# Decoder layer on one core: the last three output tiles moved one step ahead

## Chip, cores and metric

The kernel runs on one core of a Trainium2 chip. The metric is device time in microseconds (us). Besides the timed runs there is one profiled execution, from which the rows and stretches below are read. TensorE is called PE in the profile, VectorE DVE, ScalarE ACT, GpSimd POOL and SyncE SP.

## What is computed

One post-norm decoder layer for x of (2, 512, 1024), that is 1024 rows in 8 tiles of 128 rows:

```python
x = _layernorm(x + attention(x, wq, wk, wv, wo))       # 32 query heads, 8 key/value heads, window of 128
x = _layernorm(x + matmul(fake_quant(x), fake_quant(ctx)))   # "cross product"; quantised to 0..255
x = _layernorm(x + ffn(x, w_gate, w_up, w_down))       # gate and up products, truncated, down product
```

The change sits where the attention's output product (`@ wo.T`) of the last head group ends, and the first layernorm, the quantised cross product and the second layernorm follow.

## The kernel before

Each engine has its program written out by hand, and engines wait for one another with semaphores; each engine works through its own list in order. After the last attention group the 8 row tiles go through a pipeline of steps that the code calls slots: `slot(2)` to `slot(13)`. Each of the four compute engines has its own function `slot(i)`.

**TensorE**, L1224 and on. `out_tile(t)` is the last head group's output product of tile t: 24 matmuls of 128x512 in float32 (two halves of 12, L1118 to L1120), into PSUM banks 6 and 7. Its half waits until VectorE has added the same half of the tile before (`y_added`). `turn_x2(t)` transposes the second layernorm's result (8 transposes, L1220), `turn_quantised(t)` the quantised rows (8, L1188), and `cross(t)` makes the sums over each row (8 matmuls of one column, L1201) and then the cross product (16 matmuls in bf16, L1207). In slot i stand, in this order, `out_tile(i+1)` (slots 3 to 6), `turn_x2(i-6)` (from 6), `turn_quantised(i-2)` and `cross(i-3)`. So output tiles 4, 5, 6 and 7 stand in slots 3, 4, 5 and 6. From slot 11 on, parts of the feed-forward's gate and up products (L1284, L1285) stand between the slots, and behind slot 13 these products follow one another.

**VectorE**, L2765 and on. In slot i: `cross_add(i-4)` (L2718, waits for `cross(i-4)`), the small steps of the first layernorm's scale for tile i-1 (`ln_link(0, i-1, ...)`), among them the statistics of the second layernorm of tile i-4 (`ln_half(1, i-4, ...)`, L2679, and `ln_variance`), then `add_half(i+1, half)` for both halves (L2499, slots 3 to 6), the small steps of tile i-4 (from L2697), the first layernorm's statistics of tile i (which wait for its adds) and `round_rows(i-1)` (L2711). From slot 10 on `mix_columns(i-6)` (L2744 to L2751) is behind that.

**ScalarE**, `slot(i)` to slot 5 and `fast_slot(i)` from 6. In slot 6: `root(1, 2)` (L1719, waits for the variance from VectorE), `normed(0, 5)` (L1725, waits for the first layernorm's scale), `left_high(0)` (L1770, copies what `turn_x2(0)` made), `row_shift(3)` (L1749, waits for the row sums of `cross(3)`), `scale_rows(5)` (L1736), `copy_turned(4)` (L1742), `left_whole(0)` (L1774), `root(0, 6)` and `normed(1, 2)`. In slot 7 `left_high(1)` and `copy_turned(5)` stand first, then `root(1, 3)`, `normed(0, 6)`, `row_shift(4)`, `scale_rows(6)`, `left_whole(1)`, `root(0, 7)` and `normed(1, 3)`. `turn_x2(1)` on TensorE waits for `left_whole(0)`, which frees the banks that it writes. `round_rows(5)` on VectorE waits for `scale_rows(5)`.

**GpSimd** in slot i: `quantise_rows(i-2)` (L2208, waits for `round_rows(i-2)`; `turn_quantised(i-2)` on TensorE waits for it), `xb_l` of tile i-7 (L2224, from slot 7), the context's sums added to tile i-2 (L2244), and the row shift added to tile i-3 (L2250, waits for `row_shift(i-3)`; `cross_add(i-3)` waits for it).

**SyncE** waits for all output products (`wo_done`) before it loads `jw`, stores each finished tile of the second layernorm (`keep_x2`) and loads the weights of the feed-forward behind these stores.

Slot 6 and later stand in a branch (`FIRST_SLOT = 6`), which is chosen by a value that VectorE makes in slot 3.

Of the kernel before, what the change touches and what calls it, by code (L numbers as in the profile page):

```python
# [18 lines left out]
TILES = TOK // P  # L19
# [12 lines left out]
NH = DM // HALF  # L32
# [38 lines left out]
def build(nc, x_rows, x_cols, w_att, ctx_rows, x1_scale, x1_zp, x2_scale, x2_zp, w_gu, w_down, out):  # L71
    with ExitStack() as stack:
# [609 lines left out]
        def ln_of(k, t):  # L682


            return ln[:, k % 2 * 2 + t % 2, :]
# [297 lines left out]
        def _(pe):  # L983
# [128 lines left out]
            def out_product(m, into, t, half):  # L1112

                b, rows = t // TPB, slice(t % TPB * P, (t % TPB + 1) * P)
                for h in range(GROUP):
                    oh = o_h[b][:, h, rows]
                    ol = o_l[b][:, h, rows]
                    pe.matmul(into, oh, wo_h[half][:, h, :], start=(h == 0), stop=False)  # L1118
                    pe.matmul(into, oh, wo_l[half][:, h, :], start=False, stop=False)  # L1119
                    last = pe.matmul(into, ol, wo_h[half][:, h, :], start=False, stop=(h == GROUP - 1))  # L1120
                last.then_inc(wo_done, 1)
# [18 lines left out]
            def out_tile(t):  # L1140

                if t == TPB:
                    pe.wait_ge(o_low, HKV * UNITS)
                for half in range(NH):
                    m = OUT_BLOCKS - 2 * (TILES - t) + half
                    pe.wait_ge(y_added, m - 1)
                    out_product(m, y_ps[1 + half], t, half)
# [34 lines left out]
            def turn_quantised(t):  # L1182
                pe.wait_ge(x_quant, t + 1)
                if t == 0:
                    pe.wait_ge(p_low, HKV * UNITS)
                wait(pe, xq_ready, t)
                for c in range(DC):
                    last = pe.transpose(turned_bf[:, c * P:(c + 1) * P], x_q[:, t % 2, c * P:(c + 1) * P], ident_bf[:, :])  # L1188
                last.then_inc(xq_turned, 1)

            def cross(t):

                pe.wait_ge(xq_ready, t + 1)
                if t == 0:
                    pe.wait_ge(o_low, HKV * UNITS)
                    pe.wait_ge(y_added, OUT_BLOCKS - 12)
                    pe.wait_ge(sum_ready, 1)
                    pe.wait_ge(path_chosen, 1)
                wait(pe, shift_ready, t)
                for c in range(KC):  # L1200
                    last = pe.matmul(bank(5)[:, 0:1], x_qt[:, t % 2, c, :], ones_bf[:, 0:1],  # L1201
                                     start=(c == 0), stop=(c == KC - 1))
                last.then_inc(rows_summed, 1)
                wait(pe, cross_added, t)
                for half in range(NH):
                    for c in range(KC):
                        last = pe.matmul(bank(half), x_qt[:, t % 2, c, :],  # L1207
                                         ctx_quantised((t // TPB) * KC + c)[:, half * HALF:(half + 1) * HALF],
                                         start=(c == 0), stop=(c == KC - 1))
                last.then_inc(cross_done, 1)  # L1210

            def turn_x2(t, general):
                pe.wait_ge(ln_done[1], t + 1)
                wait(pe, x2_copied, t if general else min(t, TPB))
                if not general:
                    wait(pe, x2_taken, t - TPB)
                if t == 0:
                    pe.wait_ge(sum_ready, BATCH)
                for c in range(DC):
                    last = pe.transpose(bank(2 + c // 4)[:, (c % 4) * P:(c % 4 + 1) * P],  # L1220
                                        resid[:, t, c * P:(c + 1) * P], ident[:, :])
                last.then_inc(x2_turned, 1)

            def slot(i, general=False):  # L1224


                if 3 <= i < TILES - 1:
                    out_tile(i + 1)
                if 6 <= i < TILES + 6:
                    turn_x2(i - 6, general)  # L1230
                if 2 <= i < TILES + 2:
                    turn_quantised(i - 2)
                if 3 <= i < TILES + 3:
                    cross(i - 3)
# [33 lines left out]
            out_tile(3)  # L1268
            values_pair(g, 6)
            slot(2)  # L1270
            sum_context(1, 0)
            sum_context(1, 1)
# [1083 lines left out]
        def _(dve):  # L2356
# [139 lines left out]
            def add_product(m, source, t, half):  # L2496
                cols = slice(half * HALF, (half + 1) * HALF)
                dve.wait_ge(wo_done, m + 1)
                dve.tensor_tensor(resid[:, t, cols], source, resid[:, t, cols], ALU.add).then_inc(y_added, 1)  # L2499
# [9 lines left out]
            def add_half(t, half):  # L2509
                add_product(OUT_BLOCKS - 2 * (TILES - t) + half, y_ps[1 + half], t, half)  # L2510
# [178 lines left out]
            def ln_link(k, t, i):  # L2689

                if 0 <= t < TILES:
                    small = ln_of(k, t)
                    mean, var, root, r0 = small[:, 12:13], small[:, 14:15], small[:, 15:16], small[:, 16:17]
                    sq, corr, inv, offset = small[:, 17:18], small[:, 18:19], small[:, 19:20], small[:, 20:21]
                    if i == 0:
                        dve.wait_ge(ln_root[k], t + 1)
                        dve.reciprocal(r0, root).then_inc(ln_step[k], 1)  # L2697
                    else:
                        dve.wait_ge(ln_step[k], t * LN_STEPS + 3 + i)
                    if i == 1:  # L2700
                        dve.tensor_scalar(sq, r0, r0, var, ALU.mult, ALU.mult).then_inc(ln_step[k], 1)
                    if i == 2:
                        dve.tensor_scalar(corr, sq, -0.5, 1.5, ALU.mult, ALU.add).then_inc(ln_step[k], 1)
                    if i == 3:
                        dve.tensor_scalar(inv, r0, corr, None, ALU.mult).then_inc(ln_step[k], 1)
                    if i == 4:
                        dve.tensor_scalar(offset, mean, inv, -1.0, ALU.mult, ALU.mult).then_inc(ln_scale[k], 1)
# [6 lines left out]
            def cross_add(t):  # L2714

                dve.wait_ge(cross_done, t + 1)
                dve.wait_ge(x1_moved, t + 1)
                dve.scalar_tensor_tensor(out=resid[:, t, :], in0=ps[:, 0:2, :].rearrange("p a n -> p (a n)"),  # L2718
                                         scalar=param(S12), in1=resid[:, t, :], op0=ALU.mult,
                                         op1=ALU.add).then_inc(cross_added, 1)  # L2720
                dve.wait_ge(cross_added, t + 1)

            def choose_path():

                dve.wait_ge(misfit_sum, 1)
                dve.tensor_scalar(general[:, :], bank(0)[:, 0:1], 1.0, None, ALU.min).then_inc(path_chosen, 1)
# [30 lines left out]
            def slot(i, general=False):  # L2757

                if i == 3:
                    choose_path()  # L2760
                if 4 <= i < TILES + 4:
                    cross_add(i - 4)
                ln_link(0, i - 1, 0)
                ln_half(1, i - 4, 0)
                ln_link(0, i - 1, 1)  # L2765
                ln_half(1, i - 4, 1)
                ln_link(0, i - 1, 2)
                ln_variance(1, i - 4)
                if i == 3:
                    context_sums(1)  # L2770
                ln_link(0, i - 1, 3)
                for half in range(NH):
                    if 3 <= i < TILES - 1:
                        add_half(i + 1, half)
                    if half == 0:
                        ln_link(0, i - 1, 4)
                ln_link(1, i - 4, 0)
                if i < TILES:
                    dve.wait_ge(y_added, TILE_ADDED[i])
                ln_half(0, i, 0)  # L2780
                ln_link(1, i - 4, 1)
                ln_half(0, i, 1)
                ln_link(1, i - 4, 2)
                ln_variance(0, i)
                ln_link(1, i - 4, 3)
                ln_link(1, i - 4, 4)
                if 1 <= i < TILES + 1:
                    round_rows(i - 1)
                if general and LOW_BY_POOL + 6 <= i < TILES + 6:
                    columns_low(i - 6)  # L2790
                if not general and TPB + 6 <= i < TILES + 6:
                    mix_columns(i - 6)
# [335 lines left out]
```

## Time and profile before

| | |
|---|---|
| median of 3 runs | 1472.59 us (1471.60 to 1473.77) |
| profiled execution, its own time | 1474.21 us |
| its span, first to last instruction | 1472.5 us |
| TensorE busy | 1431.7 us (97%) |
| VectorE busy | 1002.9 us (68%) |
| ScalarE busy | 791.0 us (54%) |
| GpSimd busy | 740.1 us (50%) |
| mean granted clock of TensorE | 0.995 |

Busy shares are means over the whole span. The span is made of stages with different limits; the slots of the change take about 90 us of it, from 1027 to 1117 us. All times below that look like 1061.21 are counted from the start of the span. A row of the timeline is: start in us, length in us, engine, line, operation, what it writes and reads, how many of them follow one another, and in square brackets how long the engine had been idle before it and which instruction ended that. Matmuls overlap, so a group's length is a little over its distance to the next.

### The profile page before, as it was taken

To read this page: it belongs to the slowest core of one execution; us is meant where nothing else is said; L and a number is where in the kernel's file an instruction comes from. 1 tells how busy PE (TensorE), PEld (TensorE's weight loads), DVE (VectorE), ACT (ScalarE), POOL (GpSimd) and SP (SyncE) were. 2 spreads that over 40 slices of the span, in tenths; PEclk is the share of its full clock that TensorE was granted. 3 is DMA by queue.
4 is the path that set the end of the run, shared out by engine and by line. 5 is a ranking of instruction groups with operands and counts; after the bars stand their busy time and mean duration, and the time that the engine had idled before them with its cause. 6 is when DMAs were issued, how large, how long until landed. Compare 5 with 4: busy or idle time off the path is not lost.

```text
span 1472.5 us, 22884 instructions
## 1 busy us (share of the span) xinstructions
PE 1431.7 (97%) x7072; PEld 1158.4 (79%) x7088; DVE 1002.9 (68%) x1768; ACT 791.0 (54%) x1561; POOL 740.1 (50%) x651
## 2 busy tenths in 40 slices
PE   8899999999999999999999999999979999999996
PEld 6688888888888888888888888887648888778643
DVE  7644444445555578888888888887787656556596
ACT  5433333333345465657566666674576555555674
POOL 0477777777566445555555555553475333443100
PEclk9999999999999999999999999999999999999998
DMA  6378777777662757576767676671131222122611
GB/s 228 140 272 285 285 282 268 275 273 261 208 236 101 297 181 280 178 264 195 269 205 264 217 256 230 223 267 76 38 149 59 93 100 87 70 92 86 230 43 73
DMA packets 105882, 281.10 MB, mean 191 GB/s; under 512 B 12768, under 2 KB 13152, under 8 KB 105824
## 3 DMA queue, kind: packets, MB, share of 16 engines
q1 hardware_dynamic: 105824, 280.41, 54.1%
q8 instruction: 27, 0.44, 0.1%
q14 instruction: 31, 0.25, 0.1%
HBM read 184.94 MB, written 95.42 MB: 190 GB/s over the span
## 4 chain that ended last, share of the span: by engine, by line
PE 54%; DVE 6%; ACT 3%; issue 2%; DMA 2%; POOL 1%; SPq 1%; DVEq 0%; ACTq 0%; POOLq 0%
PE ps L1118 8%; PE ps L1120 7%; PE ps L1119 7%; PE ps L1284 6%; PE ps L1285 6%; PE ps L1337 5%; PE ps L1048 2%; PE ps L1047 2%; PE ps L1049 2%; PE ps L1060 2%; PE ps L1095 2%; PE ps L1094 2%; PE ps L1096 2%; PE ps L1207 1%; DVE u_val L2829 1%
## 5 line engine op out<-in xcount | busy, mean ns | idle before, releaser
L1028 PE MATMUL ps<-xo_h,wb_h 128*128 128x512 f32 x644 | 251.6, 391 | 6.0 <-ACT c L1502 2.8
L1029 PE MATMUL ps<-xo_l,wb_h 128*128 128x512 f32 x644 | 250.7, 389 | 0.0
L1030 PE MATMUL ps<-xo_h,wb_l 128*128 128x512 f32 x644 | 250.7, 389 | 0.0
L1118 PE MATMUL ps<-wo_h,o_h 128*128 128x512 f32 x512 | 207.9, 406 | 1.8 <-DMA wo_l<-wo_low 1.8
L1120 PE MATMUL ps<-wo_h,o_l 128*128 128x512 f32 x512 | 200.3, 391 | 0.0
L1119 PE MATMUL ps<-wo_l,o_h 128*128 128x512 f32 x512 | 200.1, 391 | 0.0
L2156 POOL TENSOR_TENSOR pm_l<-pt_l,upto 128x512 fp32r<-128x512 f32 x58 | 74.8, 1290 | 230.4 <-DVE pt_l L2480 230.4
L1497 ACT ACTIVATE wb_h<-wf_l 128x512 fp32r<-128x512 f32 x69 | 43.6, 632 | 197.8 <-DVE wf_l L2409 82.3
L1028 PEld LDWEIGHTS ps<-xo_h,wb_h 128*128 128x128 f32 x644 | 120.9, 188 | 33.8 <-issue 6.0
L2121 POOL TENSOR_TENSOR wb_l<-wf_l,wb_h 128x512 fp32r<-128x512 f32 x66 | 88.8, 1346 | 112.8 <-DVE s_sum L2404 56.8
L1546 ACT ACTIVATE prob<-prob,exp_bias 128x128 f32<-128x128 f32 x256 | 99.8, 391 | 83.5 <-DVE exp_bias L2467 83.5
L1030 PEld LDWEIGHTS ps<-xo_h,wb_l 128*128 128x128 f32 x644 | 120.9, 188 | 25.4
L1029 PEld LDWEIGHTS ps<-xo_l,wb_h 128*128 128x128 f32 x644 | 120.9, 188 | 24.6
L2121 POOL TENSOR_TENSOR wb_l<-raw,wb_h 128x512 fp32r<-128x512 f32 x66 | 88.1, 1336 | 62.5 <-DVE wb_l L2393 48.5
L1120 PEld LDWEIGHTS ps<-wo_h,o_l 128*128 128x128 f32 x512 | 96.1, 188 | 21.5
L1118 PEld LDWEIGHTS ps<-wo_h,o_h 128*128 128x128 f32 x512 | 96.5, 188 | 19.2 <-DMA wo_l<-wo_low 1.3
L2499 DVE TENSOR_TENSOR resid<-ps,resid 128x512 f32<-128x512 f32 x128 | 87.5, 684 | 32.7 <-PE ps L1120 31.3
L1119 PEld LDWEIGHTS ps<-wo_l,o_h 128*128 128x128 f32 x512 | 96.6, 189 | 16.5
L2137 POOL TENSOR_TENSOR q_l<-q_raw,q_h 128x512 fp32r<-128x512 f32 x64 | 83.1, 1298 | 16.3 <-ACT q_h L1524 16.3
L1284 PE MATMUL ps<-t_h,ws 128*128 128x512 f32 x228 | 88.7, 389 | 0.0
L1285 PE MATMUL ps<-t_l,ws 128*128 128x512 f32 x228 | 88.7, 389 | 0.0
L2132 POOL TENSOR_TENSOR wp_l<-wp_raw,wp_h 128x1024 fp32r<-128x1024 f32 x32 | 76.8, 2400 | 0.0
(262 smaller groups left out, 3579.0 us busy)
## 6 DMA issues: line engine op xcount, KB each, us to landing
raw<-w_att SPq DMA_DIRECT2D x47, 512.0 KB, 5.4
f_raw<-w_gu SPq DMA_DIRECT2D x44, 512.0 KB, 5.0
u_gu<-f_unit SPq DMA_DIRECT2D x42, 512.0 KB, 5.0
gq<-u_gu SPq DMA_DIRECT2D x42, 512.0 KB, 3.8
wp_raw<-w_att SPq DMA_DIRECT2D x32, 512.0 KB, 5.9
wo_high<-wp_h SPq DMA_DIRECT2D x32, 512.0 KB, 2.8
wo_low<-wp_l SPq DMA_DIRECT2D x32, 512.0 KB, 4.1
q_rows<-c SPq DMA_DIRECT2D x64, 256.0 KB, 2.9
```

The source lines that it names most:

```text
L1028: pe.matmul(prod_ps[i], wh, chunk(xo_h[i], c), start=(i in OPENS and c == 0), stop=False, skip_group_check=True)
L1029: pe.matmul(prod_ps[i], wh, chunk(xo_l[i], c), start=False, stop=False, skip_group_check=True)
L1030: last = pe.matmul(prod_ps[i], wl, chunk(xo_h[i], c), start=False, stop=(c == KH - 1), skip_group_check=True)
L1118: pe.matmul(into, oh, wo_h[half][:, h, :], start=(h == 0), stop=False)
L1119: pe.matmul(into, oh, wo_l[half][:, h, :], start=False, stop=False)
L1120: last = pe.matmul(into, ol, wo_h[half][:, h, :], start=False, stop=(h == GROUP - 1))
L1284: pe.matmul(dst, w[:, c * P:(c + 1) * P], chunk(xh, c), start=(start and c == 0), stop=False, skip_group_check=True)
L1285: last = pe.matmul(dst, w[:, c * P:(c + 1) * P], chunk(xl, c), start=False, stop=(c == KH - 1), skip_group_check=True)
L1546: last = act.activation(prob[:, par, a, :], prob[:, par, a, :], ACT.Exp, bias=exp_bias[:, par, a:a + 1], scale=SCALE, accum_out=row_sum[:, ...
L2121: pool.tensor_tensor(wb_l[i][:, :], weight_source(odd, i), plain(wb_h[i][:, :]), ALU.subtract).then_inc(w_low, 1)
L2137: pool.tensor_tensor(q_l[:, j % 2, :], q_raw[:, :], plain(q_h[:, j % 2, :]), ALU.subtract).then_inc(q_low, 1)
L2499: dve.tensor_tensor(resid[:, t, cols], source, resid[:, t, cols], ALU.add).then_inc(y_added, 1)
```

## The change

On TensorE slot 3 issues `out_tile(4)` and also `out_tile(5)`, slot 4 `out_tile(6)`, slot 5 `out_tile(7)`, and slot 6 none. On VectorE slot 3 adds tile 4 where it did, and tile 5 a little further down; slots 4 and 5 add tiles 6 and 7 there, behind the first small step of the second layernorm; slot 6 adds none. ScalarE, GpSimd and SyncE keep their programs. The number of instructions, their shapes and the buffers are the same.

```diff
@@ TensorE, slot(i) @@
-                if 3 <= i < TILES - 1:
-                    out_tile(i + 1)
+                if i == 3:
+                    out_tile(4)
+                if 3 <= i < TILES - 2:
+                    out_tile(i + 2)
                 if 6 <= i < TILES + 6:
                     turn_x2(i - 6, general)
@@ VectorE, slot(i) @@
                 for half in range(NH):
-                    if 3 <= i < TILES - 1:
-                        add_half(i + 1, half)
+                    if i == 3:
+                        add_half(4, half)
                     if half == 0:
                         ln_link(0, i - 1, 4)
                 ln_link(1, i - 4, 0)
+                if 3 <= i < TILES - 2:
+                    for half in range(NH):
+                        add_half(i + 2, half)
                 if i < TILES:
                     dve.wait_ge(y_added, TILE_ADDED[i])
                 ln_half(0, i, 0)
```

## Rows read from the trace of the kernel before

**Rows 1.** The page, busy time of each engine.
```profile
PE 1431.7 (97%) x7072; PEld 1158.4 (79%) x7088; DVE 1002.9 (68%) x1768; ACT 791.0 (54%) x1561; POOL 740.1 (50%) x651
```

**Rows 2.** PE's waits, 1000 to 1250 us: total, times, longest.
```profile
PE ps L1220 <- DVE x_l L2751: 4.3, 2, 3.9
PE ps L1220 <- ACT xb_raw L1774: 3.8, 3, 1.9
PE ps L1188 <- POOL x_q L2208: 0.4, 1, 0.4
```

**Rows 3.** Chain that ended last, in order of time: start, us, what.
```profile
1062.95 3.41 PE ps L1207 x15
1066.38 1.29 DVE resid L2718
...
1071.45 1.14 ACT x_scaled L1736
...
1074.40 2.36 POOL xb_l L2224
...
1083.02 4.78 PE ps L1207 x15
```

**Rows 4.** Timeline of PE: out_tile(4) with what follows, out_tile(7), slots 6, 7, 12.
```profile
1026.92 0.48 PE L1118 MATMUL ps<-wo_h,o_h 128*128 128x512 f32 x1
...
1032.47 0.62 PE L1188 MATMUL ps<-ident_bf,x_q 128*128 128x128 bf16 x8
...
1055.55 0.58 PE L1118 MATMUL ps<-wo_h,o_h 128*128 128x512 f32 x1
...
1061.21 1.03 PE L1220 MATMUL ps<-ident,resid 128*128 128x128 f32 x8
...
1066.56 1.06 PE L1220 MATMUL ps<-ident,resid 128*128 128x128 f32 x8 [0.21 <-ACT xb_raw L1774]
...
1105.48 1.23 PE L1220 MATMUL ps<-ident,resid 128*128 128x128 f32 x8 [3.91 <-DVE x_l L2751]
```

**Rows 5.** Timeline of DVE, slots 5 to 8.
```profile
1054.67 0.68 DVE L2711 TENSOR_SCALAR x_scaled<-x_scaled 128x1024 f32<-128x1024 f32 x1
1055.94 1.28 DVE L2718 SCALAR_TENSOR_TENSOR resid<-ps,prm,resid 128x1024 f32<-128x1024 f32 x1 [0.58 <-PE ps L1207]
...
1066.38 1.28 DVE L2718 SCALAR_TENSOR_TENSOR resid<-ps,prm,resid 128x1024 f32<-128x1024 f32 x1 [1.07 <-PE ps L1207]
...
1069.95 0.15 DVE L2697 RECIPROCAL ln<-ln 128x1 f32<-128x1 f32 x1
...
1072.62 0.69 DVE L2711 TENSOR_SCALAR x_scaled<-x_scaled 128x1024 f32<-128x1024 f32 x1 [0.34 <-ACT x_scaled L1736]
1073.23 1.28 DVE L2718 SCALAR_TENSOR_TENSOR resid<-ps,prm,resid 128x1024 f32<-128x1024 f32 x1
```

**Rows 6.** Timeline of ACT, slots 6 and 7.
```profile
1059.26 0.20 ACT L1719 ACTIVATE ln<-ln 128x1 f32<-128x1 f32 x1 [3.22 <-DVE ln L2687]
...
1062.28 1.02 ACT L1770 ACTIVATE xb_h<-ps 128x1024 fp32r<-128x1024 f32 x1 [0.94 <-PE ps L1220]
...
1063.35 1.24 ACT L1736 ACTIVATE x_scaled<-resid,prm 128x1024 f32<-128x1024 f32 x1
...
1065.38 1.03 ACT L1774 ACTIVATE xb_raw<-ps 128x1024 f32<-128x1024 f32 x1
...
1067.66 1.02 ACT L1770 ACTIVATE xb_h<-ps 128x1024 fp32r<-128x1024 f32 x1
...
1069.69 0.20 ACT L1719 ACTIVATE ln<-ln 128x1 f32<-128x1 f32 x1
1070.07 1.24 ACT L1725 ACTIVATE resid<-resid,ln 128x1024 f32<-128x1024 f32 x1 [0.17 <-DVE ln L2707]
...
1074.74 1.02 ACT L1770 ACTIVATE xb_h<-ps 128x1024 fp32r<-128x1024 f32 x1
```

**Rows 7.** Timeline of POOL: quantise_rows(4).
```profile
1055.44 1.05 POOL L2208 TENSOR_SCALAR x_q<-x_scaled 128x1024 bf16<-128x1024 f32 x1 [1.49 <-DVE x_scaled L2711]
```

**Rows 8.** Busy by stretch: PE, PEld, DVE, ACT, POOL, PE's granted clock, DMA share, GB/s.
```profile
1083.00:1086.00 3.00, 2.98 (x8) 1.16 (x8) 1.62 (x8) 2.78 (x5) 3.00 (x2) 0.54 0.46 171
...
1105.50:1110.00 4.50, 4.50 (x17) 3.79 (x18) 3.19 (x4) 2.18 (x4) 4.50 (x3) 0.62 0.00 0
```

## Prediction

> **What bounds the kernel now.** I read the page first: TensorE is busy for 97% of the span [rows 1], so time can only be won or lost in its few idle stretches or in what it must do. The change moves no work between engines and adds none, so the question is what it does to TensorE's idle time. The second view is the list of TensorE's waits around the change: from 1000 to 1250 us there are some 8.5 us of them, nearly all in front of `turn_x2`, for ScalarE's copy that frees its banks and for VectorE's `mix_columns`, and one for GpSimd's quantised rows [rows 2]. None falls before 1061 us: slots 3 to 5 are dense on TensorE. The third view is the chain that ended last. It stays on TensorE through `cross(3)`, leaves it at 1066.38 us for VectorE's `cross_add(3)`, and then runs over ScalarE's `scale_rows(6)` and GpSimd's `xb_l` back to TensorE's `cross(6)` at 1083.02 us [rows 3]. So up to slot 6 TensorE sets the pace, and in slots 7 to 12 the other three do. From `turn_x2(6)` at 1105.48 us on, before which it waited 3.91 us [rows 4], TensorE is dense again. What is late at that point is late at the end, and what is early there is won. The timelines of slots 6 and 7 [rows 4 to 7] then give the step.
>
> **Slots 3 to 5, TensorE.** An output tile takes 5.55 us (1026.92 to 1032.47) [rows 4]. The 24 matmuls of `out_tile(5)` go in front of `cross(0)`, so `cross(0)`, `cross(1)` and `cross(2)` each end about 5.5 us later. I take 5.5. No wait appears there, by my reading: `out_tile(5)` needs tile 4's first half added, an add that VectorE can make while TensorE is on the second half. When `out_tile(7)` is done, TensorE has done the same instructions in both versions, so `turn_x2(0)` starts at 1061.2 us as it does now [rows 4]. For TensorE alone the swap costs nothing and brings nothing; its cover is that these slots have no waits.
>
> **Slots 4 to 6, VectorE.** Its adds wait for the output tiles and its `cross_add` for the cross products, so its slots 4 and 5 keep their pattern and lie 5.5 us later. `cross_add(2)`, which opens slot 6, moves from 1055.94 [rows 5] to 1061.4. `round_rows(4)` moves from 1054.67 [rows 5] to 1060.15, and `quantise_rows(4)` from 1055.44 to 1060.9 and ends at 1062.0 [rows 7], just when TensorE comes to `turn_quantised(4)` (0.9 us behind 1061.2). That costs 0 to 0.1; I take 0. `cross(3)` then ends near 1066.3 as now.
>
> Slot 6 of VectorE has no adds any more. A slot without adds is slot 7, from 1066.38: ScalarE's `root(1, 3)` follows 3.31 us behind its start (1069.69), `normed(0, 6)` 3.69 us (1070.07), and its `round_rows` would be at 5.83 (5.90, unless ScalarE is late; it stood at 6.24 with 0.34 of waiting) [rows 5, 6]. I use 3.69 and 5.9.
>
> **Slot 6, ScalarE: here the change costs.** Now `root(1, 2)` starts at 1059.26 and `normed(0, 5)` just behind it, both before TensorE's transposes are there, and `left_high(0)` follows at 1062.28 [rows 6]. After the change `normed(0, 5)` can't start before 1061.4 + 3.69 = 1065.1. ScalarE's list is fixed, so `left_high(0)`, `row_shift(3)`, `scale_rows(5)`, `copy_turned(4)` and `left_whole(0)` queue up behind it. With `normed` taking 1.24 [rows 6], `left_high(0)` starts at 1065.1 + 1.24 = 1066.33: 1066.33 - 1062.28 = 4.05 us later. From there to slot 7's `left_high(1)` at 1067.66 ScalarE is dense, so everything in it is 4.05 us later: `scale_rows(5)` starts at 1067.4 and ends at 1068.64; `left_whole(0)` starts at 1069.4; `left_high(1)` at 1071.7. Who waits: `turn_x2(1)` on TensorE goes from 1066.56 to 1070.6, so TensorE sits idle from 1066.2 for some 4.4 us (now 0.21) [rows 4]; `round_rows(5)` goes to 1068.7, so `cross_add(3)` is at 1069.3 against 1066.38 [rows 5], 2.9 us later.
>
> **Slot 7 brings the two delays together.** `root(1, 3)` stands behind `left_high(1)` and `copy_turned(5)`: 1071.7 + 1.82 = 1073.5. VectorE needs it 3.57 us into its slot (1069.95 - 1066.38) [rows 5], that is at 1072.9, and waits. ScalarE's `normed(0, 6)`, on the other hand, need no longer wait for VectorE. Now it starts 0.38 behind `root(1, 3)` [rows 6]; two that don't wait follow at about 0.12, as the root is short. So it starts at 1073.65 against 1070.07: 3.6 us later. `scale_rows(6)`, `round_rows(6)`, `cross_add(4)` (1076.8 against 1073.23 [rows 5]) and `left_high(2)` (1078.3 against 1074.74 [rows 6]) all hang on this with the pattern of now. From here both engines and GpSimd are late by one amount, the loop through the three is closed, and I see nothing in slots 8 to 12 with slack against it.
>
> **The other parts.** SyncE's `jw` load waits for the last output product, now 4 us earlier; it is used 50 us later. GpSimd's list does not change; its slot 7 work (xb_l, sums, shift) ends before `round_rows(6)` is there. Bank waits of the two output tiles back to back: 0, or at most the length of an add, under them the 5.5 us of a tile.
>
> **The sum:** 0 (slots 3 to 5) + 4.05 (slot 6, ScalarE) - 0.45 (slot 7, ScalarE's own waits on VectorE that go) = +3.6 us. Against the profiled execution's own 1474.21 that is 1477.8; it stands 1.6 above the median of the runs, so against 1472.59 it is 1476.2 us.
>
> **TensorE's clock** is a term of both signs. After the idle 3.91 us before `turn_x2(6)` the granted clock was 0.62 over the next 4.5 us, and in slot 9, behind several short waits, 0.54 over 3 us [rows 4, 8]: each a stretch at 1.2 GHz instead of 2.4. In slot 9 the 15 matmuls took 4.78 where slot 6's took 3.41 [rows 3], 1.4 us on the chain. The new idle 4.4 us can bring such a stretch into slot 7. By the same two rows it costs nothing if it ends before `turn_x2(1)`, and 1.4 or a little more, say 1.7, if all of it is on the path; its first instructions, the transposes, are on it and the cross product behind them has over 1 us of room, so I put 0.9 there as likely if it comes. On the other side, shifted waits in slot 9 may leave the clock at full and give 1.4 back. I take the two as cancelling, and keep the ends -1.4 and +1.7.
>
> The Trainium skill (TensorE: Matmul & The Clock Gate, "What's actually happening" and "HAM oscillation") says that an idle stretch that is long enough brings TensorE back to half its clock, and that sustained work must pass before it is lifted. The trace agrees in the 0.62 behind the 3.91 us [rows 4, 8]. By that rule this change speaks against itself, since it makes a gap of the same length in slot 7: the sum would be 3.6 + 0.9 = 4.5 us.
>
> **The rivals.**
> (a) The half clock falls into slot 7 and slot 9 keeps its own: +4.5, up to 3.6 + 1.7 = +5.3, so 1477.1 to 1477.9. For it: the length of the gap. Against: only what follows at once is on the path. 20%.
> (b) Not slower: TensorE stays at full clock through slots 7 and 9. Then 3.6 - 1.4 = +2.2, 1474.8 us, within 0.2%. It decides where the stretch of slot 9 goes and costs under 0.7 in slot 7. For it: slot 9's stretch came from several small waits, and these shift. Against: the pattern of the waits stays as it is. 17%.
> (c) Only VectorE counts, since ScalarE catches up: slot 6 of VectorE takes 6.5 us without waits, `cross_add(3)` stands at 1061.4 + 6.5 = 1067.9, 1.5 us later than now: 1474.1. Against it: ScalarE's list is dense for 6 us behind a start that is 5 us later. 9%.
> (d) Faster: with no output tile in slot 6, its cross product is done earlier and the slots behind gain. It would need slot 5 to end early, but that now holds the tile. The most it could bring is the 1.07 that VectorE waited for `cross(3)` [rows 5] and slot 9's 1.4, some 2.5 us or 1470; a gain over 0.2% needs more than this. 4%.
>
> **How the numbers follow.** About 0.2%, 2.9 us, is what a measurement of this kernel can tell from no change. The forecast of +3.6 (3.0 to 4.4) has 50% and (a) 20%; both lie above that bound. (b) and (c) are within 0.2%, 26%, and (d) holds 4%. The forecast is near the bound, so I move 3 of its 50 to "same". Faster 4%, same 29%, slower 67%. The range reaches from (c), 1474.0, to past (a), 1478.4.
>
> **What would show it.** In the profile after: `turn_x2(0)` near 1061 as before; `cross_add(2)` near 1061.4; ScalarE with no idle time from about 1065 to 1072; TensorE idle for about 4 us in front of `turn_x2(1)`, its wait named as ScalarE's `xb_raw`; `turn_x2(6)` near 1109. I am wrong if TensorE waits in slots 3 to 5, if `left_high(0)` is not behind `normed(0, 5)` in time, or if the delay shrinks between slots 7 and 12.

## The result: 0.28% slower

The changed kernel takes 1477.83 us (median of 13 runs, 1475.77 to 1480.05), the kernel before in the same rounds 1473.59 us. The ratio is 1.0028 with a 95% interval of [1.0021, 1.0035], that is 4.1 us with 3.1 to 5.2. The forecast was 1476.2 us, 3.6 above a median of 1472.59 for the kernel before; that median came out 1.0 higher in these rounds, so the difference is the better comparison. Differences in us are the ratio's part above 1 times the median before; one of the 11 executions of experiment 1 took 1796.67 us and is left out of its ratio.

**The profile after.** TensorE's waits from 1000 to 1250 us (engine, line, released by: total, times, longest), which answer to [rows 2]:

```profile
PE ps L1220 <- ACT xb_raw L1776: 6.4, 2, 4.1
PE ps L1220 <- DVE x_l L2753: 4.2, 2, 3.9
PE ps L1207 <- DVE resid L2720: 0.8, 2, 0.5
```

The wait for `mix_columns` is as long as it was. The wait for ScalarE's copy has grown from 3.8 to 6.4, and its longest from 1.9 to 4.1. Of the third row, 0.46 are new: `cross(3)` waits for `cross_add(2)`. The timeline of TensorE shows where (`turn_x2(0)`, `cross(3)`, `turn_x2(1)` with what follows in slot 7, and `turn_x2(6)`), beside [rows 4]:

```profile
1026.31 0.48 PE L1118 MATMUL ps<-wo_h,o_h 128*128 128x512 f32 x1
...
1060.58 1.04 PE L1220 MATMUL ps<-ident,resid 128*128 128x128 f32 x8
...
1062.69 3.63 PE L1207 MATMUL ps<-ctx_q,x_qt 128*128 128x512 bf16 x16 [0.46 <-DVE resid L2720]
1070.43 1.94 PE L1220 MATMUL ps<-ident,resid 128*128 128x128 f32 x8 [4.12 <-ACT xb_raw L1776]
1072.17 1.06 PE L1188 MATMUL ps<-ident_bf,x_q 128*128 128x128 bf16 x8
...
1073.28 4.84 PE L1207 MATMUL ps<-ctx_q,x_qt 128*128 128x512 bf16 x16
...
1109.85 1.89 PE L1220 MATMUL ps<-ident,resid 128*128 128x128 f32 x8 [3.87 <-DVE x_l L2753]
```

`turn_x2(0)` starts 34.3 us behind the start of `out_tile(4)` in both kernels (1060.58 - 1026.31 and 1061.21 - 1026.92): slots 3 to 5 cost TensorE nothing. `turn_x2(1)` then waits 4.12 us for `left_whole(0)`. Its 8 transposes take 1.94 us where [rows 4] have 1.06, and the cross product behind them 4.84.

ScalarE in slots 6 and 7, beside [rows 6]:

```profile
1064.66 0.20 ACT L1721 ACTIVATE ln<-ln 128x1 f32<-128x1 f32 x1 [3.83 <-DVE ln L2689]
1065.03 1.24 ACT L1727 ACTIVATE resid<-resid,ln 128x1024 f32<-128x1024 f32 x1 [0.17 <-DVE ln L2709]
1066.18 1.00 ACT L1772 ACTIVATE xb_h<-ps 128x1024 fp32r<-128x1024 f32 x1
...
1067.23 1.24 ACT L1738 ACTIVATE x_scaled<-resid,prm 128x1024 f32<-128x1024 f32 x1
...
1069.26 1.03 ACT L1776 ACTIVATE xb_raw<-ps 128x1024 f32<-128x1024 f32 x1
...
1072.41 1.02 ACT L1772 ACTIVATE xb_h<-ps 128x1024 fp32r<-128x1024 f32 x1 [0.91 <-PE ps L1220]
```

The list is dense from 1065.03 to 1071.5, and `left_high(0)` stands behind `normed(0, 5)`. Then `left_high(1)` waits 0.91 us for the slowed transposes of `turn_x2(1)`; in [rows 6] it waited for nothing. VectorE's `cross_add(2)` and `round_rows(5)`, and its wait for `root(1, 3)` in slot 7, beside [rows 5]:

```profile
1061.35 1.28 DVE L2720 SCALAR_TENSOR_TENSOR resid<-ps,prm,resid 128x1024 f32<-128x1024 f32 x1 [1.22 <-PE ps L1207]
...
1068.49 0.69 DVE L2713 TENSOR_SCALAR x_scaled<-x_scaled 128x1024 f32<-128x1024 f32 x1 [1.25 <-ACT x_scaled L1738]
...
1074.47 0.16 DVE L2699 RECIPROCAL ln<-ln 128x1 f32<-128x1 f32 x1 [1.66 <-ACT ln L1721]
```

**One clock for all profiles.** The profiles differ by up to 1.6 us in where slot 3 starts, so from here on times are counted from the start of `out_tile(4)`. The first five columns are the starts of `cross_add` (VectorE) in slots 6 to 10, the sixth that of `turn_x2(6)`, from which TensorE is dense; the last is its difference from the kernel before. Each is one profiled execution.

| profile | slot 6 | slot 7 | slot 8 | slot 9 | slot 10 | `turn_x2(6)` | later by |
|---|---|---|---|---|---|---|---|
| before | 29.02 | 39.46 | 46.31 | 53.73 | 60.90 | 78.56 | |
| changed | 35.04 | 42.79 | 51.85 | 58.69 | 65.88 | 83.54 | 4.98 |
| copies first | 35.02 | 41.87 | 49.30 | 56.71 | 63.75 | 81.40 | 2.84 |
| adds last | 34.71 | 42.46 | 50.58 | 57.43 | 64.63 | 82.28 | 3.72 |
| only tile 7 | 35.00 | 42.75 | 51.13 | 58.58 | 65.65 | 83.30 | 4.74 |
| filler | 35.01 | 42.77 | 50.29 | 57.70 | 64.76 | 82.42 | 3.86 |
| seven behind | 29.03 | 35.89 | 48.38 | 55.23 | 62.42 | 80.07 | 1.51 |
| rows first | 35.03 | 41.87 | 50.89 | 57.74 | 64.93 | 82.59 | 4.03 |
| branch late | 34.46 | 42.21 | 50.32 | 57.17 | 64.36 | 82.01 | 3.45 |
| both remedies | 34.47 | 41.33 | 48.76 | 56.18 | 63.23 | 80.88 | 2.32 |

The spans of the two profiles differ by 3.5 us and not by 4.98. Slot 3 started 0.6 us sooner in the changed kernel's profile (1026.31 against 1026.92). The other 0.9 lies at the end: TensorE waited 1.1 us for the DMA of `d_far` in the profile before and 0.2 in the one after. The earlier start of slot 3 lies ahead of anything that the change touches. Whether the shorter wait for the DMA comes of the change is not shown.

### The profile page after: what moved, and what is told of

The parts are those of the page before. It is cut to its first block, busy times and chain, and to the rows that moved or that the text cites. A ratio compares the mean times of both kernels' runs of the same rounds, so it can differ in the third digit from the quotient of the medians.

```text
span 1476.0 us, 22900 instructions
## 1 busy us (share of the span) xinstructions
PE 1435.3 (97%) x7088; PEld 1160.8 (79%) x7088; DVE 1001.7 (68%) x1768; ACT 790.8 (54%) x1561; POOL 739.4 (50%) x651
## 4 chain that ended last, share of the span: by engine, by line
PE 54%; DVE 6%; ACT 3%; issue 2%; DMA 2%; POOL 1%; SPq 1%; DVEq 0%; ACTq 0%; POOLq 0%
PE ps L1118 8%; PE ps L1120 7%; PE ps L1119 7%; PE ps L1286 6%; PE ps L1287 6%; PE ps L1339 5%; PE ps L1048 2%; PE ps L1047 2%; PE ps L1049 2%; PE ps L1060 2%; PE ps L1095 2%; PE ps L1094 2%; PE ps L1096 2%; PE ps L1207 1%; DVE u_val L2834 1%
```

## The experiments

All were timed in five rounds against the kernel before. The interval of an experiment's ratio is 2.6 to 3.5 us wide, so the times tell 4 us from 1, and the profiles tell where.

**1. ScalarE's copies first.** The changed kernel; only ScalarE's order in slot 6 is edited.

```diff
-                if without_out:
+                if without_out or i == 6:
                     if t < TPB:
                         left_high(t)
...
                     if i < TILES + 2:
                         copy_turned(i - 2)
+                if i == 6:
+                    left_whole(t)
                 if i < TILES + 4:
                     root(1, i - 4)
```

> The changed kernel, with one edit on ScalarE in slot 6: left_high(0), copy_turned(4) and left_whole(0) stand ahead of root(1, 2) and normed(0, 5), so that the copies of what TensorE has made no longer queue behind the late layernorm. Theory (the loss comes through ScalarE's list in slot 6, which starts at 1065.0 us and is dense from there): turn_x2(1) then starts right behind cross(3), near 1066.5 in place of 1070.4, with no idle gap and no half clock behind it; cross_add(3) near 1068; what is left is VectorE's own delay of about 1.5 us, so the kernel is 1.2 to 2.2 us slower than the one before, ratio 1.001. Rival A (ScalarE's order is no part of it, VectorE's late slot 6 alone carries the loss): ratio stays at 1.0028. Rival B (what costs is the late cross products on TensorE as such): 1.0028 as well, with turn_x2(1) early but slots 8 to 12 as late as now.

Measured: 1475.83 us against 1472.78, ratio 1.0019 [1.0010, 1.0029], so +2.8 us with 1.5 to 4.3. It is above what the theory gave (1.2 to 2.2), and the lower end of the interval lies inside. The interval holds the rivals' 1.0028 too, so the profile has to decide. TensorE in slots 6 and 7:

```profile
1066.07 1.04 PE L1220 MATMUL ps<-ident,resid 128*128 128x128 f32 x8
1069.38 0.62 PE L1188 MATMUL ps<-ident_bf,x_q 128*128 128x128 bf16 x8 [2.27 <-POOL x_q L2213]
```

`turn_x2(1)` follows `cross(3)` with no gap, as expected. What waits now is `turn_quantised(5)`, for GpSimd's rows, and these wait for `round_rows(5)`: VectorE's own lateness, and a wait that the theory had not named. `turn_x2(6)` is 2.84 us late in place of 4.98. Rival B said that the slots behind would be as late as in the change, and rival A's unchanged time needs the same; slot 8's `cross_add` starts 2.55 us sooner, and about 2 of that stays. The 2.1 us between the two profiles are not all ScalarE's list: experiment 4 puts 1.1 of them down to half clock in slot 7, which leaves 1.0 for the list.

Half clock came into slot 7 here too, against the expectation: `cross(4)` took 5.30 us where it takes 3.61 at full clock.

```profile
1070.04 5.30 PE L1207 MATMUL ps<-ctx_q,x_qt 128*128 128x512 bf16 x16
```

It cost nothing on the path: from slot 7 to slot 8 `cross_add` took 7.43 us here and 7.43 in experiment 8, where the same cross product took 3.61.

**2. VectorE's adds last.** The changed kernel, with tiles 5 to 7 added at the end of VectorE's slots.

```diff
                 ln_link(1, i - 4, 0)
-                if 3 <= i < TILES - 2:
-                    for half in range(NH):
-                        add_half(i + 2, half)
...
                     round_rows(i - 1)
+                if 3 <= i < TILES - 2:
+                    for half in range(NH):
+                        add_half(i + 2, half)
```

> The changed kernel with VectorE's adds of tiles 5, 6 and 7 at the end of slots 3, 4 and 5 (behind round_rows) in place of ahead of the first layernorm's statistics. Theory (slot 6 is opened by cross(2), which ends near 1060.6 wherever VectorE adds, since TensorE's order is unchanged): cross_add(2) stays at 1061.3 to 1061.4, ratio 1.0028 as for the change, within 0.5 us of it. Rival (the statistics of tiles 3, 4 and 5 are late because the adds stand ahead of them, and this is what slots 6 and 7 pay): slot 6 opens earlier or runs shorter and 1 to 3 us come back, ratio under 1.002.

Measured: 1477.20 us, ratio 1.0028 [1.0017, 1.0040], the same as the change. Where VectorE adds the halves does not matter; `cross_add(2)` stands 0.33 us sooner in the profile, 34.71 against 35.04, and that is the branch of experiment 7: its read here starts at 1058.4 and is over at 1060.2, while VectorE still has `round_rows(4)` and the two adds to do, so less of it is left over at the end.

**3. Only tile 7 moved.** The smaller dose, written from the kernel before.

```diff
-                if 3 <= i < TILES - 1:
+                if 3 <= i < TILES - 2:
                     out_tile(i + 1)
+                if i == TILES - 3:
+                    out_tile(TILES - 1)
```

> A smaller dose of the change: output tiles 4, 5 and 6 stay in slots 3, 4 and 5 and only tile 7 moves, from slot 6 to slot 5 (two tiles in slot 5), its adds on VectorE with it. cross(0) and cross(1) are then where they were before, only cross(2) is 5.5 us later. Theory (one late cross product, the one that opens slot 6, is all that matters): the same loss as the whole change, +3.5 to +4.7 us, ratio 1.0028. Rival (each late cross product adds its share): a third of it, +1 to +2 us, ratio 1.001.

Measured: 1476.95 us, ratio 1.0028 [1.0016, 1.0040]. One cross product that is late by a tile, the last before slot 6, costs as much as three. A third of the loss, 1.001, is excluded.

**4. A filler for the clock.** The changed kernel, with work for TensorE in the new gap. The added products go into a bank that is overwritten later; nothing of the computation is left out.

```diff
                 if 3 <= i < TILES + 3:
                     cross(i - 3)
+                if i == 6 and not general:
+                    pe.wait_ge(y_added, OUT_BLOCKS)
+                    for c in range(16):
+                        pe.matmul(bank(7), ident_bf[:, :], ctx_quantised(c)[:, 0:HALF], start=(c == 0), stop=(c == 15))
```

> The changed kernel with 16 added matmuls of 128x512 in bf16 on TensorE behind cross(3), in the gap ahead of turn_x2(1), into a bank that nobody reads before it is overwritten. They take about 3.5 us, from 1066.3 to 1069.8, and end before turn_x2(1) can start; they keep TensorE at work, so that the clock is not lowered in slot 7. Theory (the late lists cost 3.6 us, the half clock in slot 7 the rest, 0.5 to 1.2 us): turn_x2(1) takes 1.04 us in place of 1.94 and cross(4) 3.6 in place of 4.8, the kernel is +2.6 to +3.6 us against before, ratio 1.0018 to 1.0025. Rival (the half clock is most of the loss): +1 or less. Rival (VectorE and ScalarE hide the half clock): no difference, +4.2.

Measured: 1477.28 us, ratio 1.0030 [1.0019, 1.0042]. That is above the theory's 1.0018 to 1.0025 and nearest to the rival by which nothing changes; the interval holds both. That half clock is most of the loss is excluded. Whether it is a part of it the time can't tell. The profile tells more. TensorE in slot 7 of this kernel:

```profile
1070.25 1.06 PE L1220 MATMUL ps<-ident,resid 128*128 128x128 f32 x8 [0.66 <-ACT xb_raw L1780]
...
1071.80 3.61 PE L1207 MATMUL ps<-ctx_q,x_qt 128*128 128x512 bf16 x16
```

The stretch of the changed kernel over the same work (columns as in [rows 8]) shows the granted clock at half, 1.2 GHz:

```profile
1070.00:1073.50 3.50, 3.07 (x25) 2.92 (x26) 2.64 (x10) 2.59 (x5) 3.44 (x3) 0.50 0.34 139
```

At full clock `cross_add(4)` follows `cross_add(3)` by 7.52 us (filler), at half clock by 9.06 (changed). By slot 10 the difference has shrunk from 1.56 to 1.12 us, and it is 1.12 at `turn_x2(6)`: 83.54 - 82.42. The other profiles bear this out. Where the transposes of slot 7 ran at half clock (1.94 us: changed, only tile 7) `turn_x2(6)` is 4.98 and 4.74 late; where they ran at full clock and what follows them was slowed it is 4.03 late (rows first) and 3.72 (adds last, 4.05 with its head start of 0.33), about 0.2 more than the filler's 3.86. ScalarE's list shows the way: `left_high(1)` waits 0.91 us for the slowed transposes in the changed kernel and 0.90 in only tile 7, and for nothing in the other three, and `root(1, 3)` and `normed(0, 6)` stand behind it. So half clock costs the path about 1 us if it meets the transposes and some 0.2 if it comes behind them, and executions of nearly the same program differ in this.

The same profile shows what held `cross_add(6)` in slot 10, with TensorE at full clock all along. The chain of this kernel (start, us, what):

```profile
1085.02 2.36 POOL xb_l L2230
1087.38 2.32 POOL resid L2250
1089.70 1.12 POOL resid L2256
...
1090.91 1.30 DVE resid L2724
```

It is GpSimd's row shift, not the cross product. GpSimd's rows in the kernel before say the same: its row shift of tile 6 ends at 1086.47 + 1.12 = 1087.59, with `cross_add(6)` at 1087.82.

```profile
1086.47 1.12 POOL L2250 TENSOR_SCALAR resid<-resid,shift 128x1024 f32<-128x1024 f32 x1
```

The half clock in slot 9 of the kernel before was therefore hidden: from slot 9 to slot 10 it took 7.17 us with it and 7.06 in the filler's profile without it.

**5. The opposite move.** From the kernel before: `out_tile(7)` behind `cross(3)`, its adds in VectorE's slot 7, and ScalarE's order fitted to it.

```diff
@@ TensorE @@
-                if 3 <= i < TILES - 1:
+                if 3 <= i < TILES - 1 and (i < 6 or general):
                     out_tile(i + 1)
...
                     cross(i - 3)
+                if i == 6 and not general:
+                    out_tile(TILES - 1)
@@ ScalarE, fast_slot @@
+                if i == 6:
+                    root(1, 2)
+                    normed(0, 5)
+                    row_shift(3)
+                    scale_rows(5)
+                    copy_turned(4)
+                    root(0, 6)
+                    act.wait_ge(wo_done, OUT_BLOCKS)
+                    left_high(0)
+                    left_whole(0)
+                    normed(1, 2)
+                    return
-                without_out = i >= TILES - 1
+                without_out = i >= TILES
@@ VectorE @@
+                if i == 7 and not general:
+                    for half in range(NH):
+                        add_half(TILES - 1, half)
```

> The kernel before, with the last output tile moved the other way: out_tile(7) stands behind cross(3) at the end of slot 6 in place of ahead of turn_x2(0), and VectorE adds it in slot 7. ScalarE in slot 6 takes normed(0, 5), row_shift(3), scale_rows(5) and copy_turned(4) first and then, when the tile is done, left_high(0) and left_whole(0) (they overwrite its weights); in slot 7 it takes root(1, 3) and normed(0, 6) first. cross(3) then ends 5 us earlier, and cross_add(3), which waits for it and for scale_rows(5), can start at 1062.5 to 1064 in place of 1066.4. turn_x2(1) stays near 1066.5, behind the tile. Theory (ScalarE's list from slot 6 on sets the pace, and it is dense; it can start its slot 6 sooner than before only by the little that it waits there): 0.8 to 1.6 us faster than before, ratio 0.999. Rival (the end of cross(3) on TensorE alone sets the pace of the slots behind it, so that the change loses because of it and the opposite move wins the same): 3 to 4 us faster, ratio 0.9975. Rival (the work is only shifted): no difference.

Measured: 1474.46 us against 1473.74, ratio 1.0003 [0.9994, 1.0012]. I expected a gain of 0.8 to 1.6 us and saw none (the interval reaches to 0.9 us faster); the gain of 3 to 4 us that would follow if the end of `cross(3)` alone set the pace is excluded. `cross_add(3)` did start 3.6 us sooner than before (35.89 against 39.46), and `cross_add(4)` 2.1 us later (48.38 against 46.31). What came between, on ScalarE and VectorE:

```profile
1065.41 1.02 ACT L1772 ACTIVATE xb_h<-ps 128x1024 fp32r<-128x1024 f32 x1 [3.28 <-PE ps L1120]
1066.34 1.02 ACT L1776 ACTIVATE xb_raw<-ps 128x1024 f32<-128x1024 f32 x1
```

```profile
1068.61 0.16 DVE L2711 RECIPROCAL ln<-ln 128x1 f32<-128x1 f32 x1 [3.17 <-ACT ln L1721]
```

ScalarE stood idle for 3.28 us for the tile whose weights `left_high(0)` overwrites, with `normed(1, 2)` and `root(1, 3)` queued behind it, and VectorE gave 3.17 us of its lead back waiting for that root. It also has tile 7's two adds (1.27 us) in this slot, and a `round_rows(6)` of 1.60 us in place of some 0.69. My estimate had forgotten the queue behind that wait. It is the mechanism of the change once more: a late entry in ScalarE's list undoes what VectorE has. The experiment moves three things at once, so it doesn't measure what an earlier cross product alone would bring.

**6. VectorE served first.** The changed kernel; in slot 6 `scale_rows(5)` goes ahead of `left_high(0)`, and `left_whole(0)` stays at its place in time.

```diff
+                if i == 6:
+                    root(1, 2)
+                    normed(0, 5)
+                    row_shift(3)
+                    scale_rows(5)
+                    left_high(0)
+                    copy_turned(4)
+                    left_whole(0)
+                    root(0, 6)
+                    normed(1, 2)
+                    return
```

> The changed kernel, with ScalarE's slot 6 in the order root(1, 2), normed(0, 5), row_shift(3), scale_rows(5), left_high(0), copy_turned(4), left_whole(0): what VectorE waits for comes one instruction sooner, what TensorE waits for comes at the same time as in the change. Theory (the loss comes on the path left_whole(0), turn_x2(1), left_high(1), root(1, 3) through ScalarE and TensorE; VectorE's wait for scale_rows(5) is not what lasts): cross_add(3) starts 0.9 us sooner (1068.2), cross_add(4) no sooner, ratio 1.0028 as for the change. Rival (VectorE's late round_rows(5) is what lasts): 0.9 us come back, ratio 1.0022.

Measured: 1477.71 us against 1473.74, ratio 1.0027 [1.0018, 1.0036]. The times can't separate 1.0027 from 1.0022. In the profile `cross_add(3)` comes 0.92 us sooner (41.87), and right behind it VectorE waits 1.01 us for `root(0, 6)`, which stands behind `left_whole(0)` in ScalarE's list:

```profile
1070.41 0.17 DVE L2710 RECIPROCAL ln<-ln 128x1 f32<-128x1 f32 x1 [1.01 <-ACT ln L1721]
```

`cross_add(4)` is 0.96 us sooner than in the changed kernel, where I expected no difference; but here the transposes of slot 7 ran at full clock (1.06 us). Against the profile with the same clock in slot 7 (adds last, with 0.33 of head start) nothing has come back: 50.89 and 50.58 at slot 8, 4.03 and 3.72 late at `turn_x2(6)`. By these profiles what lasts goes over `left_whole(0)`, `turn_x2(1)` and ScalarE's list, not over VectorE's wait for `scale_rows(5)`.

**7. VectorE's branch later.** The chain of the changed kernel has, ahead of `cross_add(2)`, pieces of VectorE's sequencer (DVEq) that the prediction did not have; VectorE's last instruction before them ends at 1060.1:

```profile
1060.13 0.74 issue
1060.87 0.22 DVEq L690
...
1061.19 0.04 DVEq L3051
...
1061.35 1.29 DVE resid L2720
```

Line 690 reads the value that chooses the path, and line 3051 is the branch. The kernel before has the same read and branch at the same place. What differs is the read's length on VectorE and on ScalarE: count, ns (least, median, most) and start, in the kernel before and then in the changed one:

```profile
L690 DVEq TENSOR_LOAD <-general x1: 550/550/550, 1054.6 to 1054.6; - x1
L690 ACTq TENSOR_LOAD <-general x1: 484/484/484, 1054.8 to 1054.8; - x1
```

```profile
L690 DVEq TENSOR_LOAD <-general x1: 1498/1498/1498, 1059.3 to 1059.3; - x1
L690 ACTq TENSOR_LOAD <-general x1: 1277/1277/1277, 1059.6 to 1059.6; - x1
```

In both kernels the read starts about 0.1 us ahead of `round_rows(4)`, and that ends some 0.6 us ahead of `cross(2)`. A read of 0.55 us is over by then; one of 1.50 is not. Slots 6 to 9 of VectorE are the same in both paths, so it can be taken later:

```diff
-            for i in range(2, FIRST_SLOT):
+            for i in range(2, TPB + 6):
                 slot(i)
...
             with dve.If(path == 0):
-                for i in range(FIRST_SLOT, TILES + 6):
+                for i in range(TPB + 6, TILES + 6):
                     slot(i)
```

> The changed kernel, with VectorE's branch (it reads the value that chooses between the two paths, and jumps) moved from ahead of slot 6 to ahead of slot 10; slots 6 to 9 are the same in both paths. In the changed kernel the chain that ended last runs through that read: VectorE's last instruction of slot 5 ends at 1060.1, cross(2) ends near 1060.9, and cross_add(2) starts at 1061.35. Theory (the branch is a second small part of the loss, since nothing is left that hides it, and the rest is as before): cross_add(2) starts 35.04 - 0.4 = 34.6 us behind the start of out_tile(4), turn_x2(6) 0.4 to 0.6 us sooner in the profile, the time 0.3 to 0.6 us under the change's, which five rounds can hardly tell: ratio 1.0022 to 1.0028. Rival (the branch costs nothing, VectorE waits for cross(2) anyway): cross_add(2) at 35.0.

Measured: 1476.40 us against 1472.96, ratio 1.0026 [1.0016, 1.0036]; as expected the times don't tell. In the profile `cross_add(2)` starts at 34.46 in place of 35.04, 0.58 us sooner, and TensorE's cross product is now what stands in front of it:

```profile
1060.69 0.03 issue
1060.71 1.29 DVE resid L2720
```

(Ahead of these two pieces the chain has the matmuls of `cross(2)`.) The difference lasts: slots 8 to 10 are 0.26 us ahead of those of adds last, which had 0.33 of it already and the same clock in slot 7. The moved read, at 1088.3, took 0.55 us.

**8. Both remedies.** The edits of experiments 1 and 7 together.

> The changed kernel with both remedies: ScalarE's slot 6 with left_high(0), copy_turned(4) and left_whole(0) ahead of root(1, 2) and normed(0, 5), and VectorE's branch ahead of slot 10. Theory: what is left is VectorE's own late slot 6; cross_add(3) about 41.4 us behind the start of out_tile(4) (39.5 before the change, 41.9 with ScalarE's order alone), the kernel 1.2 to 2.4 us slower than before, ratio 1.0008 to 1.0016. Rival (VectorE's lateness is made up once ScalarE is served): ratio 1.000. No version of the changed order should be faster than the kernel before.

Measured: 1475.48 us against 1472.96, ratio 1.0016 [1.0007, 1.0026], at the upper end of the theory's range; 1.000 is excluded. `cross_add(3)` is at 41.33 (expected 41.4), `turn_x2(6)` is 2.32 us late. With both remedies the changed order is still slower than the kernel before, so no version to prefer came out of this study.

## Why the prediction was right

**Slots 3 to 5 cost TensorE nothing.** Right: 34.3 us from `out_tile(4)` to `turn_x2(0)` in both, and no wait in between. Experiment 3 adds that the delay in slots 3 and 4 is not what costs.

**VectorE's slot 6 is 5.5 us late.** Nearly right: 35.04 - 29.02 = 6.02. The 0.5 more is the branch's read, which experiment 7 took away (34.46). I had counted the branch nowhere. In the kernel before the read took 0.55 us and was over before `cross(2)` ended; in the changed kernel it took 1.50. Why is open. The prediction put SyncE's load of `jw`, which now comes sooner, at nothing. It is issued at 1057.60 in place of 1062.35, and VectorE's read falls into its transfer and that of the rows (DMA share 0.90 over 1059.3 to 1060.8, and 0.00 over the read in the kernel before). GpSimd's read in the kernel before fell into the same transfers and took 1.85 us, and all 13 slow reads in the profiles of the change and its variants do as well; but the moved reads of experiments 7 and 8 took 0.55 us at a DMA share of 0.73. No run moves the load of `jw` alone.

**ScalarE's slot 6 is 4.05 us late, and TensorE waits for it.** Right in place, and in size but for the branch: `normed(0, 5)` at 1065.03 (forecast 1065.1), `left_high(0)` 1066.18 (1066.33), `left_whole(0)` 1069.26 (1069.4), `turn_x2(1)` 1070.43 (1070.6) after an idle 4.12 us (4.4), `round_rows(5)` 1068.49 (1068.7). That the starts agree within 0.2 us is in part luck: slot 3 began 0.6 us sooner in this profile. Counted from `out_tile(4)` all five are 0.4 to 0.5 us later than forecast, and `left_high(0)` is 4.51 us later than before in place of 4.05. That is the branch again, and by way of it `cross(3)` ended 0.6 us late as well, where I had "as now"; the idle time of 4.12 came out near the forecast's 4.4 because both its ends moved. Experiment 6 bears out that of the path's two branches the one through TensorE lasts.

**VectorE alone would give +1.5 (rival c).** It is what is left when ScalarE and the branch are mended: experiment 8 has `cross_add(3)` 1.87 us late and `turn_x2(6)` 2.32. The mechanism was real and its price 0.8 low: slot 6 took 6.86 us where I had 6.5, and slot 7 took 7.43 where the kernel before has 6.85. It is a floor under the change, and ScalarE's list comes on top. From one profile each, the 4.98 us at `turn_x2(6)` part into 2.32 (experiment 8), 0.52 for the branch (2.84 - 2.32), 1.02 for ScalarE's list at full clock (3.86 - 2.84) and 1.12 for the half clock (4.98 - 3.86). So the step that I had as the whole cost, ScalarE's queue, is the smaller part of it: with the queue out of the way, over half of the 3.86 stays.

**From slot 8 on nothing has slack.** Right, with one exception. In the filler's profile, with TensorE at full clock, the lateness is 3.98, 3.97 and 3.86 us in slots 8 to 10 and 3.86 at `turn_x2(6)`. My +3.6 for this case was 0.3 low, and these 3.86 hold the branch, which I had left out. The exception is that half clock in slot 7 is in part made up: 1.56 us at slot 8 become 1.12 at slot 10. With it the changed kernel's lateness goes from 5.54 at slot 8 to 4.96 at slot 9, and a delay that shrinks between slots 7 and 12 was one of my signs of being wrong.

**The clock.** This term was mis-sized on one side. That half clock would come into slot 7 and cost some 0.9 was right, 1.1 in the changed kernel's profile (rival a, +4.5; the measured difference is 4.1). Behind the idle 4.12 us the granted clock was 0.50 from 1070.0 to 1073.5 us; that agrees with the Trainium skill (TensorE: Matmul & The Clock Gate, "What's actually happening"), by which an idle engine goes back to half clock. But I set against it 1.4 us that slot 9's half clock costs and could give back, and took the two as cancelling. Slot 9's costs 0.1: GpSimd's row shift ends there only 0.2 us ahead of the slowed cross product. I had read the length of the group and not asked what else `cross_add(6)` waits for; two ends within some 0.2 us of each other look in a chain like one cause. With 0.1 in place of 1.4 rival (b), the case on the other side, falls, and the sum is the filler's 3.9 and 0 to 1.1 of clock, 3.9 to 5.0 us, where the runs have 3.1 to 5.2. That interval holds the forecast's 3.6 and rival (a)'s 4.5 alike, so the time does not tell them apart; the changed kernel's profile is rival (a). That +3.6 came out inside it is in part luck: the branch and the missing offset on the clock both push up from it.

**The opposite direction.** Rival (d) put a bound of 2.5 us on what an earlier cross product could bring. Experiment 5 made it 5 us earlier and got nothing that the times show, with ScalarE's order and tile 7's adds moved as well. Whether a ScalarE order that uses the 3.28 idle us would win something was not tried.

## What to carry to other kernels

When several engines work through fixed lists in a ring, a piece of work that is moved ahead of another can cost nothing where it is put, and show its cost only where the pipeline changes its pace: here in the first slot whose pace the other engines set, not TensorE. Write down for that slot what each list has in front of the entry that others wait for; here an operand 6 us late at the head of a dense list made what stands behind it 4.5 us late, however early its other inputs were. And compare such times from a common mark in both profiles, or a shift of the whole stretch passes for agreement. And where a slow group of instructions ends a wait, look at the other operands of the waiting instruction before giving the slowness a price.

## What the runs showed of the hardware

Half clock on TensorE did not cost what the slowed group's length says: 1.4 us on a cross product cost 0.1 in slot 9, and in slot 7 1.2 to 1.4 us more on the cross product cost some 0.2 at `turn_x2(6)` and 1.7 us more in experiment 1 nothing, while half clock cost 1 us there when it caught the 8 transposes as well (1.94 us in place of 1.06). Which instructions it caught differed between profiles of nearly the same program with the same idle gap of 4.1 us.

VectorE's read of one value into a register took 0.55 us in the kernel before and 1.50 in the changed one, in the same place of its list; ScalarE's took 0.48 and 1.28. In the changed kernel VectorE went from the end of its last instruction (1060.1) over the read and the branch to the next one (1061.35) in 1.2 us. Taken away, 0.6 us of it came back; the rest was hidden behind TensorE's cross product. What makes such a read long is not shown.
